# Routed experts: every stage of the row pipeline at another distance from its tile

## What is computed

```python
topk_idx, w = _route(xf, router_w, e_bias)          # 8 experts of 64 for each of 8192 tokens
order = jnp.argsort(topk_idx.reshape(-1), stable=True)
tok = order // K
sorted_x = xf[tok]                                    # 65536 rows of 512
g = jax.lax.ragged_dot(sorted_x, gate_w, group_sizes)
u = jax.lax.ragged_dot(sorted_x, up_w, group_sizes)
h = jax.nn.silu(g) * u                                # 256 hidden columns
o = jax.lax.ragged_dot(h, down_w, group_sizes)
routed = zeros.at[tok].add(o * w[order][:, None])     # added to the shared expert's output
```

## Time and profile before

| | us |
|---|---|
| median of 3 runs | 3,968.76 (3,964.9 to 3,973.75) |
| the profiled execution | 3,965.72 |
| its span, first to last instruction | 3,964.0 |
| TensorE busy in the span | 3,733.3 |
| VectorE, ScalarE, GpSimd busy | 2,235.7, 1,495.3, 1,946.4 |

### The profile page before, as it was taken

The page is one execution under the profiler, slowest core; times in us unless marked ns, Lnnn a source line. Parts: engine busy times, 40 slices in busy tenths (PEclk is TensorE's granted clock), DMA queues, the critical chain, the costliest instruction groups (busy, mean ns, idle before and its releaser), DMA issues.

```text
span 3964.0 us, 91393 instructions
## 1 busy us (share of the span) xinstructions
PE 3733.3 (94%) x17024; PEld 3040.4 (77%) x17025; DVE 2235.7 (56%) x4612; ACT 1495.3 (38%) x3339; POOL 1946.4 (49%) x1601
## 2 busy tenths in 40 slices
PE   7999999999999959999999999999999999999987
PEld 5877877878787848878878878787878778777775
DVE  4655555555555645555555555555555555566554
ACT  3222222222222214444444444444444444444443
POOL 1453333333333425655556556555656555555554
PEclk9999999999999979999999999999999999999998
DMA  5121112112111228888889888988888898899887
GB/s 181 51 57 44 44 54 54 44 44 65 44 44 54 44 70 181 182 196 177 177 191 184 182 189 182 200 176 188 178 190 185 187 201 175 194 204 204 198 185 158
DMA packets 589051, 550.56 MB, mean 139 GB/s; under 512 B 133625, under 2 KB 443265, under 8 KB 588929
## 3 DMA queue, kind: packets, MB, share of 16 engines
q0 software_dynamic: 136112, 281.38, 36.5%
q10 hardware_dynamic: 291584, 140.58, 13.9%
q1 hardware_dynamic: 161234, 127.04, 11.7%
HBM read 229.07 MB, written 179.19 MB: 103 GB/s over the span
## 4 chain that ended last, share of the span: by engine, by line
PE 46%; DMA 7%; issue 4%; ACTq 3%; DVE 2%; SPq 1%; DVEq 1%; ACT 1%; POOLq 0%; POOL 0%
PE bank L1231 30%; PE bank L1249 14%; DMA x_split<-x_rows 4%; PE bank L1240 2%; ACTq L1341 2%; DMA raw_d<-in_L_ffn_down_w_dram 1%; DMA out_dram<-o_rows,to_row 1%; DVE w_dn_l L30 1%; DMA lists<-slot_list 1%; DMA x_rows<-y_rows,from_row 1%; DVE x_cols L1407 0%; ACTq L1074 0%; SPq L1074 0%; ACT x_h L1289 0%; DVE w_gu_l L30 0%
## 5 line engine op out<-in xcount | busy, mean ns | idle before, releaser
L1193 POOL DMA_INDIRECT out_dram<-o_rows,to_row x532 | 879.5, 1653 | 278.2 <-issue 230.0
L1177 POOL DMA_INDIRECT x_rows<-y_rows,from_row x539 | 543.9, 1009 | 840.6 <-DMA x_split<-x_rows 605.5
L428 POOL DMA_INDIRECT slot_list<-ent,pos x512 | 503.9, 984 | 862.7 <-PE bank L454 385.4
L1231 PE MATMUL bank<-w_gu_h,x_h 128*128 x2128 | 844.3, 397 | 86.1 <-DVE x_l L30 42.7
L1231 PE MATMUL bank<-w_gu_h,x_l 128*128 x2128 | 840.3, 395 | 0.0
L1231 PE MATMUL bank<-w_gu_l,x_h 128*128 x2128 | 839.7, 395 | 0.0
L1407 DVE STREAM_TRANSPOSE x_cols<-x_split 128x512 f32<-128x512 f32 x535 | 580.1, 1084 | 293.9 <-DMA x_split<-x_rows 293.2
L1414 DVE TENSOR_TENSOR e_hf<-bank,e_sg 128x256 f32<-128x256 f32 x532 | 225.2, 423 | 684.4 <-ACT e_sg L1295 366.2
L1231 PEld LDWEIGHTS bank<-w_gu_h,x_h 128*128 128x128 f32 x2128 | 406.4, 191 | 186.4 <-issue 99.1
L1249 PE MATMUL bank<-w_dn_h,e_h_h 128*128 x1064 | 468.1, 440 | 33.7 <-DVE e_h_l L30 20.5
L1231 PEld LDWEIGHTS bank<-w_gu_l,x_h 128*128 128x128 f32 x2128 | 406.9, 191 | 86.7
(11 more groups left out here) (242 smaller groups left out, 5946.7 us busy)
## 6 DMA issues: line engine op xcount, KB each, us to landing
x_split<-x_rows ACTq DMA_DIRECT2D x1072, 128.0 KB
xin<-in_x_dram SPq DMA_DIRECT2D x16, 1024.0 KB
y_rows<-yrow SPq DMA_DIRECT2D x64, 256.0 KB
stage_d<-in_x_dram SPq DMA_DIRECT2D x16, 1024.0 KB
out_dram<-stage_d SPq DMA_DIRECT2D x16, 1024.0 KB
raw_gu<-in_L_ffn_gate_w_dram SPq DMA_DIRECT2D x29, 512.0 KB
raw_gu<-in_L_ffn_up_w_dram SPq DMA_DIRECT2D x29, 512.0 KB
raw_d<-in_L_ffn_down_w_dram SPq DMA_DIRECT2D x29, 512.0 KB
```

The source lines that it names most:

```text
L428: nc.gpsimd.indirect_dma_start(slots, bass.IndirectOffsetOnAxis(ap=pos[v][:, t, k:k + 1], axis=0), ent[v][:, t, k, :], None).then_inc(scat ...
L1177: nc.gpsimd.indirect_dma_start(xg[u // 2][:, u % 2, :], None, y_rows, bass.IndirectOffsetOnAxis(ap=from_row[u][:].bitcast(U32), axis=0)).t ...
L1193: nc.gpsimd.indirect_dma_start(out, bass.IndirectOffsetOnAxis(ap=to_row[u][:].bitcast(U32), axis=0), og[u][:], None, compute_op=ALU.add).t ...
L1231: last = nc.tensor.matmul(b_gu[u % 2][:], xp[a][:, u % 2, k, :], wgu[b][:, bass.ds(place, 1), k, :].rearrange("p a n -> p (a n)"), start=( ...
```

## The change

The distances at which the stages run ahead of their tile are set anew. Spreads move from the even to the odd steps and from tile j+4 to j+5 (pairs stay the same, the first step of a turn no longer has one, pair (4, 5) is spread ahead of the loop). Gathers move from j+7 to j+8, row numbers from j+8 to j+9. SP's step is written from the tile in work: list j+12, weights j+6, so that weights now follow list n by n-6 instead of n-4. SP's loop ends with the other engines' and has its first two turns unrolled; at its end it waits for the last spreads, and `load_list` has one more nop.

```diff
-            AHEAD = UN
+            LIST_AHEAD, SPREAD_AHEAD, LOAD_AHEAD = 12, 5, 6
@@ load_list
                         sp.wait_ge(list_ld[u], 16 * g)
+                        sp.nop(nofuse=True)
@@ SP
-                def step(g, u, is_first):
-                    n = g * UN + u
-                    load_list(n, u, g)
-                    weights(n - AHEAD, is_first)
+                def step(g, u, turn):
+                    j = g * UN + u
+                    load_list(j + LIST_AHEAD, (u + LIST_AHEAD) % UN, g + (u + LIST_AHEAD) // UN)
+                    weights(j + LOAD_AHEAD, turn.first(u + LOAD_AHEAD - UN))
...
-                for n in range(1, UN):
+                for n in range(1, LOAD_AHEAD):
                     weights(n, field(sp, n, 3, 1))
-                for n in range(2 * UN, LISTS):
+                for n in range(2 * UN, LIST_AHEAD):
                     load_list(n, n % UN, n // UN)
-                    weights(n - AHEAD, field(sp, n - AHEAD, 3, 1))
+                sp.wait_ge(words, 1)
+                for g in range(2):
+                    turn = Turn(sp, g + 1)
+                    for u in range(UN):
+                        step(g, u, turn)
                 last_turn = field(sp, 0, 5, NTURN - 1)
-                sp.wait_ge(words, 1)
-                with sp.Fori(LISTS // UN, NTURN + 2) as g:
-                    with sp.If(last_turn >= g - 2):
-                        turn = Turn(sp, g - 1)
+                with sp.Fori(2, NTURN) as g:
+                    with sp.If(last_turn >= g):
+                        turn = Turn(sp, g + 1)
                         for u in range(UN):
-                            step(g, u, turn.first(u))
+                            step(g, u, turn)
...
+                for v in range(UN // 2):
+                    sp.wait_ge(x_moved[v], 16 * QD * last_turn + 16 * QD * (3 - v))
                     sp.nop(nofuse=True)
@@ GpSimd
-                    gather(g + 1 + (u + 3) // UN, (u + 3) % UN)
+                    gather(g + 2, u)
...
-                for n in range(UN + 3):
+                for n in range(2 * UN):
                     gather(n // UN, n % UN)
@@ ScalarE
-                    if u % 2 == 0:
-                        spread(j + UN, u // 2, g + 1)
+                    if u % 2 == 1:
+                        spread(j + SPREAD_AHEAD, (u + SPREAD_AHEAD) % UN // 2, g + (u + SPREAD_AHEAD) // UN)
...
                 x_high(1, 1)
+                spread(UN, 0, 1)
@@ VectorE
-                    rows_from(j + 2 * UN, u, g + 2)
+                    rows_from(j + 2 * UN + 1, (u + 1) % UN, g + 2 + (u + 1) // UN)
...
                 turn_x(2, 2, 0)
+                rows_from(2 * UN, 0, 2)
```

More of the change, by code:

```diff
@@ L1152, in _ @@
                     load_list(n, n - UN, 1)
-                for n in range(1, UN):
+                for n in range(1, LOAD_AHEAD):
                     weights(n, field(sp, n, 3, 1))
-                for n in range(2 * UN, LISTS):
+                for n in range(2 * UN, LIST_AHEAD):
                     load_list(n, n % UN, n // UN)
-                    weights(n - AHEAD, field(sp, n - AHEAD, 3, 1))
+                sp.wait_ge(words, 1)
[3 more added lines that the diff above has]
+                        step(g, u, turn)
                 last_turn = field(sp, 0, 5, NTURN - 1)
-                sp.wait_ge(words, 1)
-                with sp.Fori(LISTS // UN, NTURN + 2) as g:
-                    with sp.If(last_turn >= g - 2):
-                        turn = Turn(sp, g - 1)
+                with sp.Fori(2, NTURN) as g:
+                    with sp.If(last_turn >= g):
+                        turn = Turn(sp, g + 1)
                         for u in range(UN):
-                            step(g, u, turn.first(u))
+                            step(g, u, turn)
                 for u in range(UN):
-                    sp.wait_ge(list_ld[u], 16 * last_turn + 48)
+                    sp.wait_ge(list_ld[u], 16 * last_turn + 16 * (1 + LIST_AHEAD // UN))
+                    sp.nop(nofuse=True)
+                for v in range(UN // 2):
+                    sp.wait_ge(x_moved[v], 16 * QD * last_turn + 16 * QD * (3 - v))
                     sp.nop(nofuse=True)
@@ L1216, in _ @@
                 for u in range(UN):
-                    pool.wait_ge(x_ld[u], 16 * last_turn + (48 if u < 3 else 32))
+                    pool.wait_ge(x_ld[u], 16 * last_turn + 48)
                 for u in range(UN):
```

## The result

The changed kernel takes 4,031.0 us (median of four runs, 4,025.2 to 4,035.4) against 3,969.4 for the kernel before on the same chip: a ratio of 1.0154, with a 95% interval of 1.0135 to 1.0174. It is slower by about 61 us, beyond the forecast's range. The profiled execution took 4,035.4 us, its span is 4,033.8.

What follows compares the result with a forecast made beforehand. TensorE was taken as the bound, with only its gaps to win. Pairs +12, farther loads -3, scattered losses -8 and start +1 gave +2: 3,968 against the profiled execution, 3,971 against the runs' median; range 3,915 to 3,997 us.

Steps and rivals of the forecast that it cites:

- What bounds: TensorE, busy 94% of the span: only its gaps, 162 us in the routed stage, can be won.
- the spread's gain: Spreads go out one tile, 4.33 us, earlier: at most one tile for each of 14 groups, 61 us.
- Weights: Loads go out two tiles later; nine single pairs lose 12.3 us each, 111 us against 99: +12.
- rival B: Second loads land slowly, seen at ScalarE's start_weights; single pairs lose 15.2 us each: 3,997 us, chance 0.30.
- I take 0: VectorE asks for lists one tile sooner, hidden behind the casts: no cost, bound 4.33 us per pair.
- rival A: Loads are in time; single pairs lose 6.4 us each, 51 us won: 3,918 us, chance 0.33.
- Moved, not added: Each spread's four issues, about 0.65 us each on ScalarE's queue, change place without being added.
- The scattered losses: Some 16 us from GpSimd's serial scatters at an expert's start; 8 us of them won: -8.
- +1 at their very start: ScalarE spreads pair (4, 5) ahead of the first silu: +1 us, bounds 0 and 4.
- Farther loads: Groups of loads at greater distance: -6 at tile 515, three others 1 us later each, net -3.
- Rival C: Spread isn't earlier, as ScalarE waits for the second gather at the odd step: 3,969 us, no change, chance 0.09.
- a gap in a step without a load: Sign against the forecast: it falls if a step without a load stops TensorE.

Runs made afterwards that it cites:

- e8: Kernel before with 32 list tables, lists 28 tiles ahead, spreads and loads as before: 3,960.9 us, ratio 1.000.
- e7: Changed kernel with spreads five tiles ahead on even steps, loads eight tiles ahead and 32 lists 28 tiles ahead: 3,909.4 us, ratio 0.987.
- e2: Kernel before with weights loaded six tiles ahead instead of eight: 3,997.7 us.
- e9: e7 with loads six tiles ahead instead of eight: 3,940.2 us, ratio 0.9969.
- e5: Changed kernel with 32 list tables instead of 16, lists 28 tiles ahead instead of 12, weights still six ahead: 3,994.5 us, ratio 1.0088.
- e6: e5 with weights loaded eight tiles ahead instead of six: 3,946.2 us, ratio 0.9965.
- e3: Changed kernel with spread pairs shifted one tile, so spreads five tiles ahead fall on even steps: 3,995.3 us.
- e1: Changed kernel with weights loaded eight tiles ahead instead of six: 4,024.8 us.
- e4: Changed kernel with spreads five tiles ahead on even steps and weights eight tiles ahead: 3,998.7 us.
- e11: e7 with four unused chained copies on ScalarE at the end of step 3: 3,959.5 us, ratio 0.9999.
- e12: e7 with the same four unused copies as e11, at the end of step 1 instead of step 3: 3,917.1 us, ratio 0.9888.
- e10: e6 with step 3's spread issued behind the sigmoid of the next turn's step 0, four tiles ahead of use: 4,045.7 us, ratio 1.0234.

## Why the prediction was wrong

**What bounds, and the spread's gain: right.** VectorE's wait for x_split went from 272 us to none, and where nothing else was late the tile in hand gave 51 us (e8 to e7), within what was put at "at most one tile for each of 14 groups, 61 us".

**Weights: right in kind, short in size.** The wait at start_weights came where it was put. ScalarE's and TensorE's timelines of the changed kernel at the first pair, whose loads go out at 1766.61 and 1777.24:

```profile
1775.25 1.47 ACT L1322 CAST w_gu_h<-raw_gu  x1 [5.21 <-DMA raw_gu<-in_L_ffn_up_w_dram]
...
1785.12 1.47 ACT L1322 CAST w_gu_h<-raw_gu  x1 [3.53 <-DMA raw_gu<-in_L_ffn_up_w_dram]
```

```profile
1777.51 0.44 PE L1247 MATMUL bank<-ident,e_hf 128*128 128x128 f32 x2 [2.51 <-DVE e_hf L1422]
...
1779.90 0.62 PE L1256 MATMUL bank<-w_dn_l,e_h_h 128*128 x1
...
1783.29 0.79 PE L1238 MATMUL bank<-w_gu_h,x_h 128*128 x1 [2.34 <-DVE w_dn_l L30]
...
1793.43 0.71 PE L1238 MATMUL bank<-w_gu_h,x_h 128*128 x1 [2.76 <-DVE w_dn_l L30]
```

PE(66) is 1772.12, so PE(67) on time were 1776.45. From the cast to TensorE it is 8.04 and 8.31 us (8.05 and 9.1 forecast). But the first load goes out 9.8 us ahead of PE(67) on time instead of 11.4, and its gate and up take 8.6 us instead of the estimated 7.4. PE(67) is 6.8 us late (4.1 forecast), PE(68) 12.6 (11.9). The nine pairs lose 130 us, 14.4 each, where I had 12.3 and rival B 15.2: +28 instead of +12. Over the nine pairs the second expert's cast starts 6.3 to 11.7 us after its load's issue, 8.8 in the mean, where the sum had 7.4; the four pairs above 9 us lose 16.2 to 18.3 us each, the other five 10.0 to 14.5. That is B's mechanism, slow second loads, at nearly B's price, and B alone gives 3,997. (The queues' shares in the earlier trace rows show that weights and spreads moved side by side, not in which order the DMA engines served them.) The price of the distance by itself was 24 us in the kernel before (e2) and 39 to 49 with 32 lists (e9 to e7, e5 to e6).

**"I take 0" for the lists: this step failed.** I had seen that lists stand behind a load's wait and that rows_from asks a tile sooner, and argued that the casts hide it. They do in the changed kernel's pairs, which lose 130 us with 16 lists and with 32 (e5); the ring as a whole costs 26 us there (e5) and 36 to 76 in the other three pairs of kernels (e3 to e9, e1 to e6, e4 to e7). In the changed kernel from 1510 to 1720 GpSimd waits 44.3 us in 7 places for from_row, where the kernel before has no such wait:

```profile
POOL x_rows L1184 <- DVE from_row L1405: 44.3, 7, 6.5
DVE e_hf L1422 <- ACT e_sg L1302: 44.1, 22, 4.1
...
ACT e_sg L1302 <- remote: 23.1, 10, 3.8
...
DVE from_row L1405 <- DMA lists<-slot_list: 2.3, 5, 0.6
```

A gather waits for from_row, scatters stand behind the gather, the list of n waits for the scatter of n-16, and from_row for the list: as I read it, a ring with next to no slack left. VectorE itself waits only 2.3 us for lists there, so from_row is mostly late because VectorE is, behind its waits for the sigmoid; ten of the sigmoids were released by a signal that the profile puts down to nobody ("remote"). With 32 lists the stretch has 963 matmuls instead of 906. The list's slack also decides what an earlier load is worth: at most 13 us (e1) or nothing (e4) with 16 lists, 39 to 49 with 32. My rival A, "the loads are in time", was for that reason not the kernel that I had described: with loads in time the lists are late.

**"Moved, not added" for the spread's issues: this step failed.** The count is the same, and the cost isn't, for they were moved to the end of step 3, ahead of branch, word and the next sigmoid. The sigmoid of step 0 went from in time to 1.8 us late in the median of the turns. Undoing that alone is worth 38 us (e3), and 23 to 47 in the other three pairs of kernels (e1 to e4, e6 to e7, e5 to e9), and e11 against e12 shows that ScalarE's time at that place is the cause, whatever fills it.

**The two together.** With either cure the undisturbed stretch is nearly as before: 906 matmuls in the changed kernel, 967 in e3, 963 in e5, 970 before. It would be easy to read from this that a late sigmoid and lists without slack stop TensorE only together. But e1 has both, differs from the changed kernel in the load's distance alone, no load falls in the stretch, and it holds 960. The window of e1, columns as in the earlier trace rows:

```profile
1510.00:1720.00 210.00, 208.90 (x960) 170.19 (x959) 119.10 (x241) 92.63 (x240) 127.60 (x97) 1.00 0.91 179
```

GpSimd waits 0.3 us for from_row there, not 44.3. So both faults are present in e1 without this loss, and something that no run isolates tips the changed kernel into it; the start of each kernel is also seen in one execution only. Outside this stretch each fault costs by itself: the late sigmoid 38 us with 32 lists (e6 to e7), the short ring 36 and 76 us with the sigmoid in time (e3 to e9, e4 to e7). The scattered losses, put at -8, came to +22; the tiles up to 63, for which the sum had only +1 at their very start, to +21. The shares therefore don't add up to one split of the 61 us, and I give none: by the ratio, the steps are worth 0.006 to 0.012, the lists 0.007 to 0.019, the loads nothing to 0.012, each depending on the other two, and against them stands the spread's gain of 0.013.

**Farther loads**, put at -3, came to +4 (48 to 52 in the table, 44 in e5); no run takes them apart. **Rival C** (the spread isn't earlier) is refuted by the first wait.

The forecast that a gap in a step without a load would make it fall was the right one to write down: 43 of the 75 us lie outside the groups of loads. What stays open is what starts the losses in the undisturbed stretch and how the ring of gather, scatter, list and from_row would keep such a delay: they are gone in e1, e3 and e5, after three different edits.

## What to carry to other kernels

When issues are moved on an engine's queue, price the place: add what stands behind them up to the next instruction that somebody waits for, the loop's branch and its word included; "as many as before" is no price. When a request is moved ahead, follow the ring that feeds it (here the list tables) to the oldest event it waits for, and lengthen the ring by as much as the request moved. A wait that vanishes without a gain (e1, e4) has usually uncovered the next one: cure both before judging either, as e7 did, which keeps the change's earlier spread and gives back what it took from lists, weights and the turn.

## What the runs showed of the hardware

Four DMA issues on ScalarE's queue take 2.7 us of its program, 0.65 us each, and nothing behind them starts meanwhile (e10: x_high 2.79 us later), although the transfers themselves go on behind the last issue (10.33 us). A loop's branch with the reading of one word from SBUF takes, in the median of the changed kernel's turns, 1.9 us from the last issue to the next instruction, where it is 0.3 us behind the issues of step 1; behind copies instead of issues it is 0.9 us (e11). A period is 17.3 us for four tiles. ScalarE took 2.6 us more work per turn in one step at a change of the ratio from 0.9870 to 0.9888, and in another at a change to 0.9999, while it was busy some 1,360 of 2,400 us: its busy share says nothing of its slack. In the changed kernel's first pair TensorE idled 2.51 us and then 0.92 us ahead of 1778.88; from 1779.9 a matmul takes 0.63 us instead of 0.39, and the granted clock is the lower one (1.2 GHz) from 1779.9 to 1783.0. So the fall came before the next idle time, of 2.34 us, and not behind it:

```profile
1779.90:1783.00 3.10, 1.05 (x3) 0.33 (x1) 3.05 (x3) 0.81 (x2) 0.00 (x0) 0.50 1.04 303
```
